# Quadrant layout of B, C and step sizes, one tile for masked scores, and a gate placed behind the second masks

## The chip, the cores and the metric

The kernel runs on one core of one Trainium2 chip. The metric is the device time of one execution in microseconds, less being better. The five engines are TensorE (PE in the rows, its weight loads PEld), VectorE (DVE), ScalarE (ACT), GpSimd (POOL) and SyncE (SP, which here only issues DMAs). They run side by side and are ordered by semaphores alone.

## The reference, cut to what matters

Token ids (64 sequences of 128) pick rows of a quantised embedding table. Then comes one block: a layer norm, an RMS norm, an input projection, a causal convolution of four taps, a scan over time, a gate, an output projection and an MLP. An int8-like linear layer ends it. All data is float32. The change is in the mixer of the block:

```
proj = x @ in_proj_w.T
zgate, u, Bc, Cc, dt = split(proj, [512, 1024, 1040, 1056])     # B, C: 16 wide, dt: 8 heads
u, Bc, Cc = silu(causal_conv4(u, Bc, Cc) + conv_b)
Bc, Cc = l2_normalised(Bc), l2_normalised(Cc)
dt = softplus(dt + dt_bias)
step: z = (z + d*(u B - A y)) / (1 + d*d*A);  y = y + d*z;  out = y . C
yout = (out + D_skip * u) * silu(zgate);  yout @ out_proj_w.T + out_proj_b
```

The scan is computed as a masked matrix product per sequence and head: queries times keys gives scores, the scores are masked to be causal, and their product with u is the output.

## The kernel before, in words

A first part streams the table through on-chip memory to find its quantisation scales (about the first 184 us). The middle part, where the change lies, works on 16 groups of G = 4 sequences (TOK = 512 tokens). A last part multiplies by the int8-like weights.

The middle part is a software pipeline of 18 turns, written out by hand per engine (`pe_turn`, `act_turn`, `dve_turn`, `pool_turn`; turns 2 to 14 are a loop). Turn g works on three groups at once: "first" is group g (normalise, project, recurrence), "second" is p = g-1 (scores, masks, scan output, gate, output projection), "third" is m = g-2 (MLP, residual). Every engine executes its list in order, so an instruction that waits holds up all that stands behind it.

What the change touches, with the lines of the profile:

- `pe_small` (a call of `project`, L600): one product with 40 weight columns (16 B, 16 C, 8 dt) and 512 tokens, for each of two 128-row halves of the contraction. The result is 40 partitions by 512 in `tb[0]`.
- `act_small_in` (L614, L616, L617), `act_small_dt` (L621, L623), `act_small_silu` (L627, L629), `act_small_norm` (L633), `act_small_rsqrt` (L638, L640) on ScalarE, and `dve_conv_small` (L649), `dve_d` (L661), `dve_bc` (L669 to L675) on VectorE: the convolution, softplus and normalisation of these rows, on 32 or 8 partitions by 512.
- `pe_ss` (L654): a product with `norm_sum` that sums squares over the 16 states, 512 columns wide.
- `sp_replicate` (L684 to L703): SyncE writes step sizes to HBM (`scan_rows`), reads them back spread over partitions (`d_rep`, 8 DMAs), then does the same for B and C (8 DMAs each). `act_rep` (L714) turns `d_rep` into X, for which the recurrence on GpSimd waits (`pool_recurrence`, L739 and L741, 64 steps of two instructions, in two halves; between the halves GpSimd computes norm factors from the statistics of L537 and L540).
- After the recurrence ScalarE squares its states (`act_squares`, L748), VectorE makes keys and queries (`dve_keys` from L762, `dve_inverse`, `dve_queries` up to L814), and TensorE makes scores (`pe_scores`, L919) for two half sets of four heads, hg = 0 and hg = 1.
- `dve_mask` (L930) multiplies the scores of one head by the causal mask into the tile `MT`; `pe_scan_out` (L944) multiplies it with u, in pairs of heads. `dve_gate` (L951 and L956) adds the skip and multiplies by the gate, for two 128-channel tiles at a time.
- Behind it on VectorE stand: `dve_row_stats` (L537, L540), `dve_gate` of tiles 2 and 3, `dve_mean3`, `dve_bc`, the convolution of u (`dve_conv_u`, L843), `dve_rms_rows` (L574), the residual `dve_x2` (L973) and `dve_rms` (L989 to L1005). ScalarE scales with that (`act_rms_rows`, L1016), and TensorE transposes the result (`pe_mlp_T`, L1022), goes on to `pe_small`, and then to the MLP (`pe_fc1` L1040 with `act_gelu` L1050, `pe_fc2` L1059).
- GpSimd adds the residual between two recurrences (`pool_residual`, L1069 and L1073).

The order on VectorE around the gate, before:

```
if second:
    dve_gate(dve, p, (0, 1))
    for hh in range(4):
        dve_mask(dve, p, 1, hh)
if nxt:
    dve_row_stats(dve, g + 1)
if second:
    dve_gate(dve, p, (2, 3))
```

Of the kernel before, what the change touches and what calls it, by code (L numbers as in the profile page):

```python
# [28 lines left out]
F32 = mybir.dt.float32  # L29
# [7 lines left out]
G = 4  # L37
# [5 lines left out]
FT = FF // P  # L43
SMALL = 2 * NST + HEADS
TAPS = 4
# [40 lines left out]
def build(nc, a, out):  # L86
    with ExitStack() as ctx:
# [326 lines left out]
        lnst = sb("lnst", [P, 8, G])  # L414
        bc = sb("bc", [SMALL, TOK])
        bsq = sb("bsq", [SMALL, TOK])
        nrm = sb("nrm", [2 * NST, TOK])
        bcd = sb("bcd", [SMALL, TOK])
        X2 = sb("X2", [P, CL, 2, LANES])
# [24 lines left out]

        scan_rows = nc.dram_tensor("scan_rows", (SMALL, TOK), F32, kind="Internal").ap()

# [161 lines left out]
        BC = slice(0, 2 * NST)  # L608
        DT = slice(2 * NST, SMALL)

        def act_small_in(act, g):
            ps = tb[0]
            act.wait_ge(small_mm.sem, small_mm.at(g))
            act.activation(bc[BC, :], ps[BC, :], ACT.Identity, bias=c("bc_bias", 0, BC), scale=c("bc_tap", TAPS - 1, BC)) \  # L614
                .then_inc(tap0.sem, 1)
            act.activation(bc[DT, :], ps[DT, :], ACT.Identity, bias=c("dt_bias", 0, DT)).then_inc(dt_in.sem, 1)  # L616
            act.activation(bsq[DT, :], ps[DT, :], ACT.Abs, bias=c("dt_bias", 0, DT)).then_inc(dt_in.sem, 1)  # L617

        def act_small_dt(act, g):
            act.wait_ge(dt_in.sem, dt_in.at(g))  # L620
            act.activation(bsq[DT, :], bsq[DT, :], ACT.Exp, scale=-1.0).then_inc(dt_act.sem, 1)  # L621
            act.wait_ge(dt_act.sem, dt_act.at(g, 1))
            act.activation(bsq[DT, :], bsq[DT, :], ACT.Ln, bias=1.0).then_inc(dt_act.sem, 1)  # L623

        def act_small_silu(act, g):
            act.wait_ge(cv.sem, cv.at(g))
            act.activation(bc[BC, :], bc[BC, :], ACT.Silu).then_inc(bc_silu.sem, 1)  # L627
            act.wait_ge(bc_silu.sem, bc_silu.at(g))
            act.activation(bsq[BC, :], bc[BC, :], ACT.Square).then_inc(bc_sq.sem, 1)  # L629

        def act_small_norm(act, g):
            act.wait_ge(ss_mm.sem, ss_mm.at(g))
            act.activation(bsq[BC, :], tb[1][BC, :], ACT.Identity, bias=c("eps6", 0, BC)).then_inc(nrm_act.sem, 1)  # L633

        def act_small_rsqrt(act, g):
            act.preload_act_table_set("natural_log_exp_and_others")
            act.wait_ge(nrm_act.sem, nrm_act.at(g, 1))
            act.activation(nrm[:], bsq[BC, :], ACT.Ln).then_inc(nrm_act.sem, 1)  # L638
            act.wait_ge(nrm_act.sem, nrm_act.at(g, 2))
            act.activation(nrm[:], nrm[:], ACT.Exp, scale=-0.5).then_inc(nrm_act.sem, 1)  # L640

        def dve_conv_small(dve, g):
            ps = tb[0][BC, :].rearrange("p (s t) -> p s t", s=G)
            acc = bc[BC, :].rearrange("p (s t) -> p s t", s=G)
            dve.wait_ge(tap0.sem, tap0.at(g))
            for i in range(1, TAPS):
                if i > 1:
                    dve.wait_ge(cv.sem, cv.at(g, i - 1))
                dve.scalar_tensor_tensor(acc[:, :, i:], ps[:, :, 0:LEN - i], c("bc_tap", TAPS - 1 - i, BC),  # L649
                                         acc[:, :, i:], ALU.mult, ALU.add).then_inc(cv.sem, 1)  # L650

        def pe_ss(pe, g):
            pe.wait_ge(bc_sq.sem, bc_sq.at(g))
            pe.matmul(tb[1][:, :], norm_sum[:], bsq[BC, :], start=True, stop=True).then_inc(ss_mm.sem, 1)  # L654

        def dve_d(dve, g):
            if since(g):

                dve.wait_ge(d_stored.sem, d_stored.at(g - 1))
            dve.wait_ge(dt_act.sem, dt_act.at(g))  # L660
            dve.scalar_tensor_tensor(bcd[DT, :], bc[DT, :], 0.0, bsq[DT, :], ALU.max, ALU.add) \  # L661
                .then_inc(d_ready.sem, 1)

        def dve_bc(dve, g):
            if since(g):
                dve.wait_ge(bc_stored.sem, bc_stored.at(g - 1))

            dve.wait_ge(nrm_act.sem, nrm_act.at(g))
            dve.scalar_tensor_tensor(bcd[BC, :], nrm[:], -0.5, nrm[:], ALU.mult, ALU.mult).then_inc(nrm_dve.sem, 1)  # L669
            dve.wait_ge(nrm_dve.sem, nrm_dve.at(g, 1))  # L670
            dve.tensor_tensor(bcd[BC, :], bsq[BC, :], bcd[BC, :], ALU.mult).then_inc(nrm_dve.sem, 1)
            dve.wait_ge(nrm_dve.sem, nrm_dve.at(g, 2))
            dve.scalar_tensor_tensor(nrm[:], bcd[BC, :], 1.5, nrm[:], ALU.add, ALU.mult).then_inc(nrm_dve.sem, 1)
            dve.wait_ge(nrm_dve.sem, nrm_dve.at(g, 3))
            dve.tensor_tensor(bcd[BC, :], bc[BC, :], nrm[:], ALU.mult).then_inc(bc_ready.sem, 1)  # L675

        def sp_replicate(sp, g):

            sp.wait_ge(d_ready.sem, d_ready.at(g))
            if since(g):  # L680

                sp.wait_ge(d_in.sem, d_in.at(g - 1))
                sp.wait_ge(x_ready.sem, x_ready.at(g - 1))
            sp.dma_start(scan_rows[DT, :], bcd[DT, :]).then_inc(d_stored.sem, 16)  # L684
            sp.wait_ge(d_stored.sem, d_stored.at(g))
            for hg in range(HG):
                for head in range(4):
                    row = 2 * NST + 4 * hg + head
# [6 lines left out]
            sp.dma_start(scan_rows[BC, :], bcd[BC, :]).then_inc(bc_stored.sem, 16)  # L695
            sp.wait_ge(bc_stored.sem, bc_stored.at(g))
            if since(g):

                sp.wait_ge(bk_ready.sem, bk_ready.at(g - 1))
                sp.wait_ge(kq.sem, kq.at(g - 1))  # L700
            for rep, row, arrived in ((b_rep, 0, b_in), (c_rep, NST, c_in)):
                for k in range(P // NST):
                    sp.dma_start(rep[k * NST:(k + 1) * NST, :], scan_rows[row:row + NST, :]).then_inc(arrived.sem, 16)  # L703

# [514 lines left out]
        def dve_turn(dve):  # L1219
            def turn(g, first, second, third, nxt):  # L1220
# [418 lines left out]
```

## Time and profile before

| What | Value |
|---|---|
| median of 3 runs | 1486.99 us (1486.4 to 1487.03) |
| the profiled execution, its own time | 1489.13 us |
| its span | 1487.3 us |
| TensorE busy | 1203.7 us (81%) |
| VectorE busy | 1205.1 us (81%) |
| ScalarE busy | 809.2 us (54%) |
| GpSimd busy | 848.8 us (57%) |
| mean granted TensorE clock | 0.932 of full speed |

The profiled execution took 1.8 us more than its span, and 2.1 us more than the median. A row of a timeline has the start in us, the time from there to the end of the last instruction merged into it, the engine, the line, the operation, output and inputs with their shapes, how many instructions, and in brackets the idle time ahead of it with what ended it. TensorE executes each float32 product as two matmul records, so the count in such a row is twice that of the calls.

### The profile page before, as it was taken

What the parts mean: (1) busy time and instruction counts of PE and PEld (TensorE: products, weight loads), DVE (VectorE), ACT (ScalarE), POOL (GpSimd) and SP (SyncE); (2) the same over time, 40 slices, a digit from 0 to 9 for tenths busy, and PEclk for the clock granted to TensorE, in tenths of its full rate; (3) what the DMA queues carried; (4) which work ended last, traced back from release to release, by engine and by line L of the source; (5) the groups of instructions that cost most, each with busy time, mean ns of one, the idle gap of its engine ahead of it and who ended that gap; (6) DMA issues with size and microseconds to landing.
All of it is one profiled execution on the core that took longest, in us unless ns stands there. A gap on an engine that the chain in (4) does not pass through costs nothing. (4 is left out here: it accounts for less than half of the span.)

```text
span 1487.3 us, 24635 instructions
## 1 busy us (share of the span) xinstructions
PE 1203.7 (81%) x6751; PEld 794.8 (53%) x6758; DVE 1205.1 (81%) x2087; ACT 809.2 (54%) x1108; POOL 848.8 (57%) x2326
## 2 busy tenths in 40 slices
PE   0693043498989999989999989999999999998767
PEld 0352011356575656565657565656566665657444
DVE  4899833688888888888888888888898988878268
ACT  4667253355647473838383838374747465641248
POOL 7860027575757576665757575757575757570100
PEclk9999987599999999999999999999999999999889
DMA  9999300000000010101000000000000000000015
GB/s 364 407 408 425 132 18 14 15 17 16 17 14 22 9 30 0 30 2 29 7 23 12 18 16 15 16 15 16 15 16 15 16 15 16 16 17 1 0 37 189
DMA packets 33811, 91.34 MB, mean 61 GB/s; under 512 B 8973, under 2 KB 17922, under 8 KB 29298
## 3 DMA queue, kind: packets, MB, share of 16 engines
q1 hardware_dynamic: 30226, 81.32, 15.4%
q0 software_dynamic: 3072, 8.39, 1.5%
q10 hardware_dynamic: 480, 1.24, 0.2%
q8 instruction: 15, 0.25, 0.1%
q14 instruction: 18, 0.15, 0.0%
HBM read 81.21 MB, written 9.70 MB: 61 GB/s over the span
## 5 line engine op out<-in xcount | busy, mean ns | idle before, releaser
L739 POOL TENSOR_TENSOR stp<-Gs,X 128x32 f32<-128x32 f32 x1024 | 290.3, 284 | 266.4 <-ACT X L714 176.7
L741 POOL TENSOR_TENSOR Gs<-Gs,stp 128x32 f32<-128x32 f32 x1024 | 298.2, 291 | 80.3
L600 PE MATMUL bank<-xT,w_in 128*128 128x512 f32 (+1 forms) x576 | 266.6, 609 | 15.0 <-DVE uT L843 8.2
L1059 PE MATMUL bank<-w_fc,gl 128*128 128x256 f32 x1024 | 238.0, 380 | 13.5 <-ACT gl L1050 13.5
L1040 PE MATMUL bank<-mT,w_fc 128*128 128x512 f32 x512 | 237.9, 603 | 1.5 <-ACT mT L1028 1.5
L1059 PEld LDWEIGHTS bank<-w_fc,gl 128*128 128x128 f32 x1024 | 192.2, 190 | 78.2 <-issue 30.1
L829 ACT ACTIVATE uT<-bank,cols 128x512 f32<-128x512 f32 x64 | 49.4, 776 | 251.6 <-PE bank L600 251.6
L600 PEld LDWEIGHTS bank<-xT,w_in 128*128 128x128 f32 (+1 forms) x576 | 103.0, 186 | 139.5 <-issue 117.4
L1040 PEld LDWEIGHTS bank<-mT,w_fc 128*128 128x128 f32 x512 | 95.6, 191 | 112.4 <-issue 106.9
L944 PE MATMUL bank<-MT,utok 128*64 128x128 f32 x1024 | 111.9, 409 | 45.5 <-DVE MT L930 45.5
L843 DVE SCALAR_TENSOR_TENSOR uT<-bank,cols,uT 128x500 f32<-128x500 f32 (+1 forms) x192 | 134.4, 730 | 2.3
L339 DVE TENSOR_TENSOR peak<-ring,peak 128x1536 f32<-128x1536 f32 (+2 forms) x67 | 115.4, 1722 | 19.9 <-ACT ring L242 18.5
L944 PEld LDWEIGHTS bank<-MT,utok 128*64 128x64 f32 x1024 | 103.5, 224 | 49.9 <-DVE MT L930 44.9
L1050 ACT ACTIVATE gl<-bank,cols 128x512 f32<-128x512 f32 x128 | 84.7, 684 | 76.3 <-PE bank L1059 67.9
L930 DVE TENSOR_TENSOR MT<-bank,causal 128x512 f32<-128x512 f32 x128 | 79.5, 683 | 49.3 <-PE bank L919 49.3
L242 ACT ACTIVATE ring<-ring 128x3072 f32<-128x3072 f32 (+3 forms) x35 | 90.8, 2598 | 51.8 <-DMA ring<-in_table 51.8
L965 PE MATMUL bank<-w_out,sz 128*128 128x256 f32 x512 | 113.8, 380 | 0.2 <-DVE sz L956 0.2
L965 PEld LDWEIGHTS bank<-w_out,sz 128*128 128x128 f32 x512 | 97.2, 190 | 20.7 <-issue 7.5
L807 DVE RECIPROCAL rm<-rm 128x1024 f32<-128x1024 f32 x16 | 104.6, 6540 | 0.0
L280 PE MATMUL bank<-ts,hot 4*128 4x256 f32 x128 | 60.4, 648 | 40.6 <-ACT hot L253 39.2
L226 POOL DMA_INDIRECT h<-in_table,ids x64 | 79.7, 1246 | 19.9 <-issue 19.2
L919 PE MATMUL bank<-Qf,Kf 32*128 32x64 f32 x2048 | 68.0, 283 | 19.7 <-ACT utok L889 13.0
(169 smaller groups left out, 1971.1 us busy)
## 6 DMA issues: line engine op xcount, KB each, us to landing
ring<-in_table SPq DMA_DIRECT2D x32, 1536.0 KB, 21.3
d_rep<-scan_rows SPq DMA_DIRECT2D x128, 64.0 KB, 2.0
out<-res SPq DMA_DIRECT2D x16, 512.0 KB, 2.9
b_rep<-scan_rows SPq DMA_DIRECT2D x128, 32.0 KB, 1.8
c_rep<-scan_rows SPq DMA_DIRECT2D x128, 32.0 KB, 1.8
w_fc<-in_w_fc SPq DMA_DIRECT2D x2, 1024.0 KB, 8.8
w_in<-in_w_in ACTq DMA_DIRECT2D x1, 1064.0 KB
h<-in_table,ids POOLq DMA_INDIRECT x64, 10.1
```

The costliest lines, as they stand in the source:

```text
L242: act.activation(ring[n % RING][0:np_, 0:nr, :], ring[n % RING][0:np_, 0:nr, :], ACT.Abs) \
L339: return dve.tensor_tensor(acc, ring[t][0:np_, r0:r0 + nr, :], acc, ALU.max)
L600: last = pe.matmul(dst, w_in[:, k, c0:c1], xT[:, k, :], start=(k == 0), stop=(k == KD - 1))
L739: pool.tensor_tensor(stp[:], Gs[:, t, ::-1, :], X2[:, t, :, :], ALU.mult).then_inc(rec.sem, 1)
L741: pool.tensor_tensor(Gs[:, t + 1, :, :], Gs[:, t, :, :], stp[:], ALU.add).then_inc(rec.sem, 1)
L807: dve.reciprocal(rm[:], rm[:]).then_inc(inverted.sem, 1)
L843: dve.scalar_tensor_tensor(acc[:, :, i:], ps[:, :, 0:LEN - i], c("u_tap", f * TAPS + TAPS - 1 - i), acc[:, :, i:], ALU.mult, ALU.add).then ...
L944: last = pe.matmul(pj[head // 2][64 * (head % 2):64 * (head % 2) + 64, j * LEN:(j + 1) * LEN], utok[:, j, head * HP:(head + 1) * HP], MT[h ...
L965: last = pe.matmul(sbk[n][:, (j % 2) * D:(j % 2 + 1) * D], sz[:, f, j * LEN:(j + 1) * LEN], w_out[:, f, :], start=(f == 0), stop=(f == UT ...
L1040: last = pe.matmul(pj[n % 4][:, :], w_fc1[:, k, n * P:(n + 1) * P], mT[:, k, :], start=(k == 0), stop=(k == KD - 1))
L1050: act.activation(gl[n % LEAD][:], pj[n % 4][:, :], ACT.Gelu_apprx_tanh, bias=c("fc1_bias", n)) \
L1059: last = pe.matmul(sbk[j // 2][:, (j % 2) * D:(j % 2 + 1) * D], gl[n % LEAD][:, j * LEN:(j + 1) * LEN], w_fc2[:, n, :], start=(n == 0 and ...
```

## The change

B, C and dt of the four sequences are put on four groups of 32 partitions, so that every tile of this chain is 128 partitions by 128 tokens instead of 32 (or 8) by 512. The projection is issued per sequence, once for the 32 columns of B and C and once for 32 columns of which 8 are dt and 24 are zeros: 16 calls of 128 columns instead of 2 of 512. The HBM buffers are laid out by sequence, so that DMAs move runs of 512 bytes instead of 2 KB. The four masked score tiles become one tile with the heads side by side. On VectorE the gate of tiles 0 and 1 moves behind the masks of the second half set.

```
-SMALL = 2 * NST + HEADS
+SMALL = 2 * NST
-        w_in = sb("w_in", [P, KD, 2 * DIN + SMALL])
+        w_in = sb("w_in", [P, KD, 2 * DIN + 2 * SMALL])
-        norm_sum = sb("norm_sum", [2 * NST, P])
+        norm_sum = sb("norm_sum", [P, P])
-        bc = sb("bc", [SMALL, TOK])
...
+        bc = sb("bc", [P, LEN])
...
-        MT = [sb(f"MT{i}", [P, G, LEN]) for i in range(4)]
+        MT = sb("MT", [P, G, 4, LEN])
-        scan_rows = nc.dram_tensor("scan_rows", (SMALL, TOK), F32, kind="Internal").ap()
+        bc_rows = nc.dram_tensor("bc_rows", (G, SMALL, LEN), F32, kind="Internal").ap()
+        d_rows = nc.dram_tensor("d_rows", (G, SMALL, LEN), F32, kind="Internal").ap()
         def pe_small(pe, g):
             pe.wait_ge(xT_ready.sem, xT_ready.at(g))
-            project(pe, tb[0][0:SMALL, :], 2 * DIN, 2 * DIN + SMALL, small_mm.sem)
+            for part in range(2):
+                c0 = 2 * DIN + part * SMALL
+                for k in range(KD):
+                    for j in range(G):
+                        last = pe.matmul(tb[part][SMALL * j:SMALL * (j + 1), 0:LEN],
+                                         w_in[:, k, c0:c0 + SMALL], xT[:, k, j * LEN:(j + 1) * LEN],
+                                         start=(k == 0), stop=(k == KD - 1), skip_group_check=True)
+            last.then_inc(small_mm.sem, 1)
-            act.activation(bsq[BC, :], bc[BC, :], ACT.Square).then_inc(bc_sq.sem, 1)
+            act.activation(bsq[:], bc[:], ACT.Square).then_inc(bc_sq.sem, 1)
...
-            pe.matmul(tb[1][:, :], norm_sum[:], bsq[BC, :], start=True, stop=True).then_inc(ss_mm.sem, 1)
+            pe.matmul(tb[1][:, LEN:2 * LEN], norm_sum[:], bsq[:], start=True, stop=True).then_inc(ss_mm.sem, 1)
-            sp.dma_start(scan_rows[DT, :], bcd[DT, :]).then_inc(d_stored.sem, 16)
+            sp.dma_start(d_rows.rearrange("j r t -> (j r) t"), dd[:]).then_inc(d_stored.sem, 16)
-                    sp.dma_start(d_rep[32 * head:32 * head + 32, hg, :],
-                                 scan_rows[row:row + 1, :].to_broadcast([32, TOK])).then_inc(d_in.sem, 16)
+                    sp.dma_start(d_rep[32 * head:32 * head + 32, hg, :].rearrange("p (j t) -> p j t", j=G),
+                                 d_rows[:, row:row + 1, :].rearrange("j r t -> r j t").to_broadcast([32, G, LEN])) \
+                        .then_inc(d_in.sem, 16)
...
-            dve.tensor_tensor(MT[hh][:], score_bank[hh][:, :].rearrange("p (j t) -> p j t", j=G),
+            dve.tensor_tensor(MT[:, :, hh, :], score_bank[hh][:, :].rearrange("p (j t) -> p j t", j=G),
...
                 if second:
-                    dve_gate(dve, p, (0, 1))
                     for hh in range(4):
                         dve_mask(dve, p, 1, hh)
+                    dve_gate(dve, p, (0, 1))
                 if nxt:
                     dve_row_stats(dve, g + 1)
```

## Rows read from the trace of the kernel before

**Rows 1.** Page, part 1: busy time, share of the span and instructions.

```profile
PE 1203.7 (81%) x6751; PEld 794.8 (53%) x6758; DVE 1205.1 (81%) x2087; ACT 809.2 (54%) x1108; POOL 848.8 (57%) x2326
```

**Rows 2.** The loop's instruction (L1128) on TensorE: count, duration, first and last start.

```profile
L1128 PEldq ALU_OP  x13: 32/32/32, 384.0 to 1244.2; - x13
```

**Rows 3.** Timeline of TensorE, 865 to 935 us, a turn of the loop.

```profile
868.99 2.01 PE L919 MATMUL bank<-Qf,Kf 32*128 32x64 f32 x64
872.41 3.48 PE L944 MATMUL bank<-MT,utok 128*64 128x128 f32 x32 [1.41 <-DVE MT L930]
...
897.61 1.09 PE L1022 MATMUL bank<-ident,xr 128*128 128x128 f32 x8
899.05 1.91 PE L600 MATMUL bank<-xT,w_in 128*40 128x512 f32 x4 [0.35 <-ACT xT L596]
900.89 7.13 PE L1040 MATMUL bank<-mT,w_fc 128*128 128x512 f32 x16
908.99 1.99 PE L1059 MATMUL bank<-w_fc,gl 128*128 128x256 f32 x8 [0.96 <-ACT gl L1050]
...
921.24 1.12 PE L654 MATMUL bank<-bsq,norm_sum 32*128 32x512 f32 x2
922.29 1.98 PE L1040 MATMUL bank<-mT,w_fc 128*128 128x512 f32 x4
...
933.81 1.46 PE L919 MATMUL bank<-Qf,Kf 32*128 32x64 f32 x44 [0.88 <-ACT utok L889]
```

**Rows 4.** Timeline of VectorE, the same turn.

```profile
871.07 2.48 DVE L930 TENSOR_TENSOR MT<-bank,causal 128x512 f32<-128x512 f32 x4
...
875.42 1.37 DVE L951 SCALAR_TENSOR_TENSOR uT<-uT,cols,bank 128x512 f32<-128x512 f32 x2
876.71 1.29 DVE L956 TENSOR_TENSOR sz<-sz,uT 128x512 f32<-128x512 f32 x2
...
878.74 0.70 DVE L669 SCALAR_TENSOR_TENSOR bcd<-nrm 32x512 f32<-32x512 f32 x1
...
890.08 0.88 DVE L973 SCALAR_TENSOR_TENSOR xl<-bank,off,xl 128x256 f32<-128x256 f32 x2 [0.26 <-PE bank L965]
...
906.97 2.24 DVE L661 SCALAR_TENSOR_TENSOR bcd<-bc,bsq 8x512 f32<-8x512 f32 x1 [0.92 <-ACT bsq L623]
911.35 1.22 DVE L762 TENSOR_TENSOR rm<-utok 128x1024 f32<-128x1024 f32 x1 [2.14 <-ACT utok L748]
...
931.46 1.46 DVE L1081 TENSOR_TENSOR h<-bank,h 128x512 f32 x2
```

**Rows 5.** Timeline of ScalarE, the same turn.

```profile
895.85 1.71 ACT L1016 ACTIVATE xr<-xl,ssq 128x256 f32<-128x256 f32 x4 [1.05 <-DVE ssq L1005]
...
901.00 0.77 ACT L614 ACTIVATE bc<-bank,cols 32x512 f32<-32x512 f32 x1 [0.54 <-PE bank L600]
...
904.37 0.63 ACT L621 ACTIVATE bsq<-bsq 8x512 f32<-8x512 f32 x1
...
908.25 1.27 ACT L1050 ACTIVATE gl<-bank,cols 128x512 f32<-128x512 f32 x2
909.40 1.91 ACT L748 ACTIVATE utok<-Gs 128x2048 f32<-128x2048 f32 x1
```

**Rows 6.** Timeline of GpSimd, the same turn.

```profile
875.59 0.20 POOL L549 TENSOR_TENSOR lnst<-mv,eps 128x4 f32<-128x4 f32 x1 [2.04 <-DVE mv L540]
...
906.32 2.34 POOL L1069 TENSOR_TENSOR h<-h,xl 128x1024 f32 x1 [0.29 <-issue]
908.84 2.61 POOL L1073 TENSOR_TENSOR h<-h,fc_b 128x1024 f32 x1 [0.17 <-issue]
```

**Rows 7.** Timeline of TensorE, 868.3 to 869 us: the last scan-output records.

```profile
867.97 1.10 PE L944 MATMUL bank<-MT,utok 128*64 128x128 f32 x10
```

**Rows 8.** Page, part 6: DMA issues, count, KB each, us to landing.

```profile
d_rep<-scan_rows SPq DMA_DIRECT2D x128, 64.0 KB, 2.0
...
out<-res SPq DMA_DIRECT2D x16, 512.0 KB, 2.9
```

More of the change, by code:

```diff
@@ L414, in build @@
         lnst = sb("lnst", [P, 8, G])
-        bc = sb("bc", [SMALL, TOK])
-        bsq = sb("bsq", [SMALL, TOK])
-        nrm = sb("nrm", [2 * NST, TOK])
-        bcd = sb("bcd", [SMALL, TOK])
+        bc = sb("bc", [P, LEN])
+        bsq = sb("bsq", [P, LEN])
+        nrm = sb("nrm", [P, LEN])
+        bcd = sb("bcd", [P, LEN])
+        dt = sb("dt", [P, LEN])
+        soft = sb("soft", [P, LEN])
+        dd = sb("dd", [P, LEN])
         X2 = sb("X2", [P, CL, 2, LANES])
@@ L611, in act_small_in @@
+            last.then_inc(small_mm.sem, 1)
         def act_small_in(act, g):
[L612 removed]
+            bc_in, dt_raw = tb[0][:, 0:LEN], tb[1][:, 0:LEN]
             act.wait_ge(small_mm.sem, small_mm.at(g))
[L614 removed]
+            act.activation(bc[:], bc_in, ACT.Identity, bias=c("bc_bias"), scale=c("bc_tap", TAPS - 1)) \
                 .then_inc(tap0.sem, 1)
[L616 removed]
@@ L617, in act_small_in @@
-            act.activation(bsq[DT, :], ps[DT, :], ACT.Abs, bias=c("dt_bias", 0, DT)).then_inc(dt_in.sem, 1)
+            act.activation(dt[:], dt_raw, ACT.Identity, bias=c("dt_bias")).then_inc(dt_in.sem, 1)
+            act.activation(soft[:], dt_raw, ACT.Abs, bias=c("dt_bias")).then_inc(dt_in.sem, 1)
         def act_small_dt(act, g):
             act.wait_ge(dt_in.sem, dt_in.at(g))
-            act.activation(bsq[DT, :], bsq[DT, :], ACT.Exp, scale=-1.0).then_inc(dt_act.sem, 1)
+            act.activation(soft[:], soft[:], ACT.Exp, scale=-1.0).then_inc(dt_act.sem, 1)
@@ L622, in act_small_dt @@
             act.wait_ge(dt_act.sem, dt_act.at(g, 1))
-            act.activation(bsq[DT, :], bsq[DT, :], ACT.Ln, bias=1.0).then_inc(dt_act.sem, 1)
+            act.activation(soft[:], soft[:], ACT.Ln, bias=1.0).then_inc(dt_act.sem, 1)
         def act_small_silu(act, g):
             act.wait_ge(cv.sem, cv.at(g))
-            act.activation(bc[BC, :], bc[BC, :], ACT.Silu).then_inc(bc_silu.sem, 1)
+            act.activation(bc[:], bc[:], ACT.Silu).then_inc(bc_silu.sem, 1)
             act.wait_ge(bc_silu.sem, bc_silu.at(g))
-            act.activation(bsq[BC, :], bc[BC, :], ACT.Square).then_inc(bc_sq.sem, 1)
+            act.activation(bsq[:], bc[:], ACT.Square).then_inc(bc_sq.sem, 1)
@@ L637, in act_small_rsqrt @@
             act.wait_ge(nrm_act.sem, nrm_act.at(g, 1))
-            act.activation(nrm[:], bsq[BC, :], ACT.Ln).then_inc(nrm_act.sem, 1)
+            act.activation(nrm[:], bsq[:], ACT.Ln).then_inc(nrm_act.sem, 1)
             act.wait_ge(nrm_act.sem, nrm_act.at(g, 2))
@@ L660, in dve_d @@
             dve.wait_ge(dt_act.sem, dt_act.at(g))
-            dve.scalar_tensor_tensor(bcd[DT, :], bc[DT, :], 0.0, bsq[DT, :], ALU.max, ALU.add) \
+            dve.scalar_tensor_tensor(dd[:], dt[:], 0.0, soft[:], ALU.max, ALU.add) \
                 .then_inc(d_ready.sem, 1)
@@ L668, in dve_bc @@
             dve.wait_ge(nrm_act.sem, nrm_act.at(g))
-            dve.scalar_tensor_tensor(bcd[BC, :], nrm[:], -0.5, nrm[:], ALU.mult, ALU.mult).then_inc(nrm_dve.sem, 1)
+            dve.scalar_tensor_tensor(bcd[:], nrm[:], -0.5, nrm[:], ALU.mult, ALU.mult).then_inc(nrm_dve.sem, 1)
             dve.wait_ge(nrm_dve.sem, nrm_dve.at(g, 1))
-            dve.tensor_tensor(bcd[BC, :], bsq[BC, :], bcd[BC, :], ALU.mult).then_inc(nrm_dve.sem, 1)
+            dve.tensor_tensor(bcd[:], bsq[:], bcd[:], ALU.mult).then_inc(nrm_dve.sem, 1)
             dve.wait_ge(nrm_dve.sem, nrm_dve.at(g, 2))
-            dve.scalar_tensor_tensor(nrm[:], bcd[BC, :], 1.5, nrm[:], ALU.add, ALU.mult).then_inc(nrm_dve.sem, 1)
+            dve.scalar_tensor_tensor(nrm[:], bcd[:], 1.5, nrm[:], ALU.add, ALU.mult).then_inc(nrm_dve.sem, 1)
             dve.wait_ge(nrm_dve.sem, nrm_dve.at(g, 3))
-            dve.tensor_tensor(bcd[BC, :], bc[BC, :], nrm[:], ALU.mult).then_inc(bc_ready.sem, 1)
+            dve.tensor_tensor(bcd[:], bc[:], nrm[:], ALU.mult).then_inc(bc_ready.sem, 1)
         def sp_replicate(sp, g):
@@ L687, in sp_replicate @@
                 for head in range(4):
-                    row = 2 * NST + 4 * hg + head
-                    sp.dma_start(d_rep[32 * head:32 * head + 32, hg, :],
-                                 scan_rows[row:row + 1, :].to_broadcast([32, TOK])).then_inc(d_in.sem, 16)
+                    row = 4 * hg + head
+                    sp.dma_start(d_rep[32 * head:32 * head + 32, hg, :].rearrange("p (j t) -> p j t", j=G),
+                                 d_rows[:, row:row + 1, :].rearrange("j r t -> r j t").to_broadcast([32, G, LEN])) \
+                        .then_inc(d_in.sem, 16)
             sp.wait_ge(bc_ready.sem, bc_ready.at(g))
@@ L694, in sp_replicate @@
                 sp.wait_ge(c_in.sem, c_in.at(g - 1))
-            sp.dma_start(scan_rows[BC, :], bcd[BC, :]).then_inc(bc_stored.sem, 16)
+            sp.dma_start(bc_rows.rearrange("j r t -> (j r) t"), bcd[:]).then_inc(bc_stored.sem, 16)
             sp.wait_ge(bc_stored.sem, bc_stored.at(g))
@@ L702, in sp_replicate @@
                 for k in range(P // NST):
-                    sp.dma_start(rep[k * NST:(k + 1) * NST, :], scan_rows[row:row + NST, :]).then_inc(arrived.sem, 16)
+                    sp.dma_start(rep[k * NST:(k + 1) * NST, :].rearrange("p (j t) -> p j t", j=G),
+                                 bc_rows[:, row:row + NST, :].rearrange("j r t -> r j t")).then_inc(arrived.sem, 16)
         def act_rep(act, g, hgs):
@@ L944, in pe_scan_out @@
                     last = pe.matmul(pj[head // 2][64 * (head % 2):64 * (head % 2) + 64, j * LEN:(j + 1) * LEN],
-                                     utok[:, j, head * HP:(head + 1) * HP], MT[hh][:, j, :], start=True, stop=True)
+                                     utok[:, j, head * HP:(head + 1) * HP], MT[:, j, hh, :], start=True, stop=True)
             last.then_inc(y_mm.sem, 1)
@@ L1598 @@
     cols["norm2"][:] = tall(f["L0_attn_norm2_w"])
-    cols["bc_tap"][0:2 * NST] = taps[DIN:]
-    cols["bc_bias"][0:2 * NST, 0] = f["L0_attn_conv_b"][DIN:]
-    cols["dt_bias"][2 * NST:SMALL, 0] = f["L0_attn_dt_bias"]
+    cols["bc_tap"][:] = np.tile(taps[DIN:], (G, 1))
+    cols["bc_bias"][:, 0] = np.tile(f["L0_attn_conv_b"][DIN:], G)
+    for j in range(G):
+        cols["dt_bias"][SMALL * j:SMALL * j + HEADS, 0] = f["L0_attn_dt_bias"]
     cols["u_tap"][:] = taps[:DIN].reshape(UT, P, TAPS).transpose(1, 0, 2).reshape(P, UT * TAPS)
@@ L1620 @@
         "ident": np.eye(P, dtype=np.float32),
-        "norm_sum": np.kron(np.eye(2, P // NST, dtype=np.float32), np.ones((NST, NST), np.float32)),
+        "norm_sum": np.kron(np.eye(P // NST, dtype=np.float32), np.ones((NST, NST), np.float32)),
         "causal": (s <= t).astype(np.float32),
-        "w_in": wide(f["L0_attn_in_proj_w"].T),
+        "w_in": wide(np.pad(f["L0_attn_in_proj_w"].T, ((0, 0), (0, SMALL - HEADS)))),
         "w_out": wide(f["L0_attn_out_proj_w"].T),
```

10 lines of the change are left out of this document (3 added, 7 removed).

## The prediction

> **What bounds the kernel now.** The page's totals name two candidates, TensorE and VectorE at 81% each [rows 1]. The loop over turns repeats every (1244.2 - 384.0) / 12 = 71.7 us [rows 2], so the 14 turns from 2 to 15 are two thirds of the span, and what one turn gains counts about 14 times. I then read one turn as four timelines side by side. TensorE is almost without gaps: it idles 1.41 us twice (masks, once per half set), 0.35, 0.96 and 0.88 us [rows 3]. So a turn shortens by work taken from TensorE, or by one of these gaps, and lengthens by whatever makes a new one.
>
> Three chains run beside TensorE. (a) From the end of the second scores (868.99 + 2.01 = 871.00) VectorE is dense to the row normalisation; it idles only 0.26 us there, before L973 [rows 4]. ScalarE then scales rows from 895.85 to 897.56 [rows 5], and TensorE transposes them at 897.61 [rows 3]. TensorE shows no gap there, but only 0.05 us separate the two: this chain has no slack. (b) From the small projection ScalarE goes through five small operations to the first gelu at 908.25 [rows 5], and its end at about 908.9 releases L1059 after the 0.96 us gap. (c) The recurrence on GpSimd leads to the squares at 909.40, the keys at 911.35 and h2 at 931.46 [rows 4, 5]. VectorE is done there at 932.9, while the first scores end near 933.81 + 2.01 = 935.8: slack 2.9 us.
>
> **The change, part by part, for one turn.**
>
> *Small projection.* Before: 4 records of 512 columns, 1.84 us from 899.05 to 900.89 [rows 3]. After: 32 records of 128 columns, in four column strips of the array. The nearest row is L944, also 128 columns wide and alternating between two strips: 32 records take 3.48 us, 109 ns each [rows 3]. That is the upper bound, +1.65 us. The lower bound is the rate of L919, where four row strips share the array: 2.01 / 64 = 31 ns a record [rows 3], 1.0 us in all, -0.85 us. I take the middle, 1.9 us, for this reason: ten records of L944 begin at 867.97 and the next line begins at 868.99 [rows 7, 3], 1.02 us, where ten times 109 ns is 1.09 us even without a change of shape between them. So the two strips do overlap at the end of the run, where no weights are left to load; in the stream, loading and multiplying seem to take turns. With four strips that would be four records per 213 ns, or 8 x 0.213 = 1.7 us. I take +0.1.
>
> The Trainium skill (TensorEngine Tiling (Array Packing), Overview) gives up to 4x for stationary operands of at most 32 columns; by that the projection would cost 3.41 / 4 = 0.9 us. Its page TensorE: Matmul & The Clock Gate, Part 3, speaks against the change: weight loads overlap running matmuls only in another row group, and here all rows are used. L944's 109 ns a record agrees with the second, not with the first.
>
> *Sum of squares.* Before 922.29 - 921.24 = 1.05 us [rows 3]. After: two records of 128 columns at 109 ns: 0.22. **-0.83**.
>
> *ScalarE.* An operation of 512 columns takes 0.63 us, one of 256 takes 1.71 / 4 = 0.43 [rows 5], so 384 columns fewer save 0.30 us. Five such operations stand between the small projection and the first gelu: it ends 1.5 us earlier, and the 0.96 us gap goes. **-0.96**. What is late next there is the end of fc1 itself, 0.5 us later than gelu would be. Silu, square, norm and rsqrt lie beside TensorE work; they cost nothing now and give nothing.
>
> *VectorE.* 512 columns take 0.70, 256 take 0.44 [rows 4]: 0.39 saved per operation. The four of `dve_bc` lie in chain (a): -1.56. The three of the small convolution and `dve_d` lie ahead of a wait of 2.14 us for the squares [rows 4] and give nothing.
>
> *The gate.* Masks of the second set start at 871.07, 0.07 us after the scores end: the gate ahead of them was all but hidden in the time TensorE needed for scan output and scores. Moved behind the masks, it leaves VectorE idle there and puts 1.37 + 1.29 = 2.66 us [rows 4] into chain (a). Behind it wait: the row statistics, and through them GpSimd's norm factors, which already idled 2.04 us for them [rows 6]; the second gate, `dve_bc`, the u convolution, L973, the row normalisation. Sum for chain (a): 2.66 - 1.56 - 0.26 (the wait before L973) = **+0.8** as a new gap before L1022. The u projection needs the first gate at 875.9; it would be done at 874.3.
>
> *GpSimd.* Its second half starts 2.6 us later, so the recurrence ends near 908.7, just before ScalarE is free for the squares. But the residual operations of 2.34 and 2.61 us [rows 6] then run from 909.0 to 914.1, over the first keys. That this costs is seen now: `dve_d` takes 2.24 us for 8 x 512 [rows 4] and ends 0.5 us after L1069 does; its size would give 0.70. Two such hits are up to 3.1 us on chain (c), whose slack of 2.9 us is down to 2.8. Bounds 0 and 3.1; I take **+0.3**. The Trainium skill (GPSIMD Engine Reference, Specifications) says that GpSimd and VectorE share their SBUF interface when a VectorE instruction has two SBUF inputs; the 2.24 us agrees.
>
> *DMAs.* On SyncE's queue the counts stay (1 + 8 + 1 + 16). Runs shrink from 2 KB to 512 B, and the step-size store grows from 16 to 64 KB. A replication lands in 2.0 us, a 512 KB store in pieces of 1 KB in 2.9 us [rows 8]; so 0 to 0.9 us more, on a chain that gets over 2 us earlier. Cover: ScalarE's gelus; gone, it would delay X and GpSimd, which has 2.04 us to spare. Nothing. *The MT tile:* same shapes read and written, nothing. *Zero columns and larger norm_sum:* 72 KB more at the start, 0.2 us.
>
> Sum per turn: 0.1 - 0.83 - 0.96 + 0.8 + 0.3 = -0.6; 14 turns: -8.3. Ahead of the first recurrence the small operations lie bare: about -2; the last turns, where the gate delays GpSimd's last recurrence, +1. Total -9: the profiled 1489.1 becomes 1480, the median, 2.1 lower, **1478 us**.
>
> **The rivals.**
>
> 1. *The strips don't overlap.* The projection costs the full 3.5 us: +1.55 on each turn, 14 x 1.55 = 22, so about 1500 us: slower. For it: the 109 ns of L944. Against: rows 7. It decides from 2.5 us for the projection on.
> 2. *Chain (a) does not bind.* If the masks' wait or shorter operations hide the gate, +0.8 and +0.3 vanish: -1.7 per turn, -24, so 1462 us. For it: VectorE's total falls. Against: the 0.05 us of slack.
> 3. *The gate's move eats everything.* VectorE saves less than reckoned and the collision costs 1.0 beyond its slack: 0.1 - 1.79 + 1.2 + 1.0 = +0.5, so 1493 us: slower.
> 4. *Strips in full parallel:* 0.9 us less per turn, 1465 us.
>
> A change of 0.2% (3 us) is what a measurement of this kernel can tell from none.
>
> **How the numbers follow.** Forecast 0.45, its own range 1471 to 1484; rival 1 0.22, rival 2 0.12, rival 3 0.13, rival 4 0.08. Faster by over 0.2%: the forecast's most (0.42), rivals 2 and 4: 0.62. Same: 0.08 (edges of the forecast and of rival 3). Slower: 0.30. The range takes in most of rivals 2 and 4 and half of rival 1: 1463 to 1500.
>
> **What the profile after would show.** The projection in 1.9 us or less (3.5 by rival 1); the sum of squares in 0.3; no gap before the first L1059; a new gap of 0.8 us before L1022, with VectorE idle near 3 us before the second masks; GpSimd waiting over 4 us for the statistics; its residual beside L762. I am wrong if the period is not near 71.1 us: above 71.7 by rivals 1 or 3, near 70 by rival 2.

## The result and the profile after

The changed kernel takes 1504.75 us in the median of four runs (1504.15 to 1508.39), the kernel before 1486.7 us. The ratio is 1.0128 (95% interval 1.0113 to 1.0143): slower by 18 us, where 9 us less were forecast, and outside the range by 5 us.

The page, parts 1 and 6, and one group of part 5 of the changed kernel (its profiled execution took 1508.39 us, span 1506.5 us):

```profile
PE 1200.8 (80%) x7199; PEld 828.4 (55%) x7206; DVE 1161.0 (77%) x2087; ACT 759.5 (50%) x1108; POOL 822.8 (55%) x2326
...
L927 PE MATMUL bank<-Qf,Kf 32*128 32x64 f32 x2048 | 95.3, 357 | 41.4 <-DVE h L1089 34.0
...
d_rep<-d_rows SPq DMA_DIRECT2D x128, 64.0 KB, 2.7
```

Every engine works less than in [rows 1], VectorE by 44 us (only TensorE's weight loads, PEld, grew, by 34 us), and yet the time grew. The loop's own instruction repeats (after the count the shortest, the median and the longest duration in ns, then the first and the last start in us):

```profile
L1136 PEldq ALU_OP  x13: 32/32/32, 376.9 to 1257.8; - x13
```

(1257.8 - 376.9) / 12 = 73.4 us against 71.7 [rows 2]. These twelve periods hold 20.7 us of the loss. The stretch ahead of them got 7.1 us shorter (2 were forecast), the one behind them 5.6 us longer (1 was forecast), and together that is the 19.2 us between the spans. The length of the first scores of a turn (L919 before, L927 now) was not in the forecast: they now wait for "DVE h L1089", the result of the MLP added to h (h2 in the prediction), and the mean record of all scores grew from 283 to 357 ns. The timeline of TensorE over one turn answers to [rows 3]:

```profile
642.75 3.19 PE L927 MATMUL bank<-Qf,Kf 32*128 32x64 f32 x64 [2.45 <-DVE h L1089]
647.33 3.35 PE L952 MATMUL bank<-MT,utok 128*64 128x128 f32 x32 [1.39 <-DVE MT L938]
...
679.82 1.09 PE L1030 MATMUL bank<-ident,xr 128*128 128x128 f32 x8 [0.67 <-ACT xr L1024]
681.27 1.08 PE L614 MATMUL bank<-xT,w_in 128*32 128x128 f32 x32 [0.36 <-ACT xT L600]
682.81 7.13 PE L1048 MATMUL bank<-mT,w_fc 128*128 128x512 f32 x16 [0.46 <-ACT mT L1036]
689.77 1.89 PE L1067 MATMUL bank<-w_fc,gl 128*128 128x256 f32 x8
...
701.83 0.39 PE L660 MATMUL bank<-bsq,norm_sum 128*128 128x128 f32 x2
702.05 1.88 PE L1048 MATMUL bank<-mT,w_fc 128*128 128x512 f32 x4
...
715.06 3.69 PE L927 MATMUL bank<-Qf,Kf 32*128 32x64 f32 x64 [2.47 <-DVE h L1089]
```

The turn of before that it is read against begins with two lines ahead of [rows 3]:

```profile
862.14 2.01 PE L919 MATMUL bank<-Qf,Kf 32*128 32x64 f32 x64 [0.91 <-ACT utok L889]
865.56 3.50 PE L944 MATMUL bank<-MT,utok 128*64 128x128 f32 x32 [1.41 <-DVE MT L930]
```

Read from start to start, the stretches differ so: first scores to first scan output +1.2 us, on to the transposes of L1030 +0.4 (in it the 0.67 us gap), projection -0.3 net of a new gap of 0.46, fc1 up to the first fc2 -1.1, sum of squares -0.8, the rest up to the next scores +1.3. Sum +0.6: this turn takes 72.3 us, where those of before take 71.7. Five turns of the loop take 74.4 to 74.8 us and one 73.8; in the five, the second scores take 3.69 us as well.

One more comparison shows where TensorE's saving went. From the end of the second scores to the end of h2's addition (L1081 before, L1089 now) it is 932.92 - 871.00 = 61.9 us before and 714.82 - 652.61 = 62.2 now. The side that TensorE waits for has not become shorter, so what TensorE saves on the way stands as a wait before the scores.

What VectorE and GpSimd do in the same turn, answering to [rows 4] and [rows 6]:

```profile
652.68 2.48 DVE L938 TENSOR_TENSOR MT<-bank,causal 128x512 f32<-128x512 f32 x4 [2.72 <-PE bank L927]
...
691.21 1.23 DVE L770 TENSOR_TENSOR rm<-utok 128x1024 f32<-128x1024 f32 x1 [3.83 <-ACT utok L756]
692.35 3.25 DVE L775 TENSOR_TENSOR Kf<-bk,Gs 128x512 f32<-128x512 f32 x1
...
713.54 1.28 DVE L1089 TENSOR_TENSOR h<-bank,h 128x512 f32 x2
```

```profile
659.71 0.20 POOL L553 TENSOR_TENSOR lnst<-mv,eps 128x4 f32<-128x4 f32 x1 [5.75 <-DVE mv L544]
...
688.85 2.36 POOL L1077 TENSOR_TENSOR h<-h,xl 128x1024 f32 x1 [0.29 <-issue]
691.39 3.25 POOL L1081 TENSOR_TENSOR h<-h,fc_b 128x1024 f32 x1 [0.17 <-issue]
```

VectorE stands idle 2.72 us ahead of the second masks, where the gate was. GpSimd waits 5.75 us for the statistics behind the gate. Its second residual addition runs from 691.39 to 694.64, and the key operation L775 from 692.35 to 695.60: both take 3.25 us. Alone they take 2.36 (the median in the run with the gate put back, below) and 1.1. The key operation ends 0.96 us after the addition does. L1089 ends at 714.8, and the scores start at once.

The last view is the granted clock in chosen stretches, first of the kernel before, then of the changed one (after the stretch and its length: busy time of PE, PEld, DVE, ACT and POOL, the granted clock, DMA share and GB/s):

```profile
865.60:868.90 3.30, 3.30 (x32) 3.22 (x32) 3.16 (x7) 0.00 (x0) 2.53 (x10) 0.52 0.00 0
869.00:871.00 2.00, 2.00 (x66) 1.87 (x64) 1.89 (x3) 0.00 (x0) 1.69 (x5) 1.00 0.00 0
```

```profile
642.75:645.90 3.15, 3.15 (x64) 3.00 (x64) 0.00 (x0) 0.20 (x1) 2.40 (x10) 0.60 0.00 0
```

In the kernel before, the scores (from 869.0) ran at the full 2.4 GHz, but the scan output in front of them, which follows a wait of 1.41 us, at 1.2 GHz. I had priced the new projection by just such a row, and had not asked for its clock. In the changed kernel, behind the wait of 2.45 us, the scores run at the low level for most of their time too: 3.19 us where 2.01 [rows 3] do at full clock.

Over twelve turns of the loop (first scores at 432.2 to first scores at 1292.0 us before, 424.4 to 1305.2 now) this gives, per turn, from the timelines and the clock record:

| Per turn | before | changed |
|---|---|---|
| period | 71.65 us | 73.39 us |
| TensorE's waits over 0.1 us | 5.0 us | 6.7 us |
| of these, before the first scores | 0.88 us | 2.47 us |
| of these, before L1022 / L1030 | 0 | 0.53 us (0.16 to 1.14) |
| first scores | 2.01 us | 3.31 us (2.67 to 3.69) |
| second scores | 2.01 us | 2.79 us (3.69 in five of twelve) |
| time at the low clock | 6.8 us | 13.1 us |

So the clock costs the two sets of scores 2.1 us a turn, which is more than the 1.6 us that the waits add.

### The profile page after: what moved, and what is told of

The parts are those of the page before. It is cut to its first block and busy times, and to the rows that moved or that the text cites. A ratio compares the mean times of both kernels' runs of the same rounds, so it can differ in the third digit from the quotient of the medians.

```text
span 1506.5 us, 25531 instructions
## 1 busy us (share of the span) xinstructions
PE 1200.8 (80%) x7199; PEld 828.4 (55%) x7206; DVE 1161.0 (77%) x2087; ACT 759.5 (50%) x1108; POOL 822.8 (55%) x2326
## 5 line engine op out<-in xcount | busy, mean ns | idle before, releaser
L747 POOL TENSOR_TENSOR stp<-Gs,X 128x32 f32<-128x32 f32 x1024 | 281.5, 275 | 240.7 <-DVE Kf L812 140.3
L749 POOL TENSOR_TENSOR Gs<-Gs,stp 128x32 f32<-128x32 f32 x1024 | 284.2, 278 | 80.3
L604 PE MATMUL bank<-xT,w_in 128*128 128x512 f32 x512 | 237.3, 612 | 7.8 <-DVE uT L851 7.4
L604 PEld LDWEIGHTS bank<-xT,w_in 128*128 128x128 f32 x512 | 98.0, 197 | 118.5 <-issue 105.0
L927 PE MATMUL bank<-Qf,Kf 32*128 32x64 f32 x2048 | 95.3, 357 | 41.4 <-DVE h L1089 34.0
L952 PEld LDWEIGHTS bank<-MT,utok 128*64 128x64 f32 x1024 | 99.4, 216 | 51.7 <-DVE MT L938 46.8
L927 PEld LDWEIGHTS bank<-Qf,Kf 32*128 32x128 f32 x2048 | 90.0, 266 | 49.7 <-issue 49.7
L553 POOL TENSOR_TENSOR lnst<-mv,eps 128x4 f32<-128x4 f32 x16 | 3.3, 203 | 172.5 <-DVE mv L544 172.5
```

What stands on the lines that cost most here:

```text
L604: last = pe.matmul(dst, w_in[:, k, c0:c1], xT[:, k, :], start=(k == 0), stop=(k == KD - 1))
L747: pool.tensor_tensor(stp[:], Gs[:, t, ::-1, :], X2[:, t, :, :], ALU.mult).then_inc(rec.sem, 1)
L749: pool.tensor_tensor(Gs[:, t + 1, :, :], Gs[:, t, :, :], stp[:], ALU.add).then_inc(rec.sem, 1)
L927: last = pe.matmul(score_bank[hh][:, t:t + CL], Kf[own, hg * G + j, ch * CL:ch * CL + P], Qf[own, hg, t:t + CL], start=True, stop=True)
```

## The experiments

Three questions: which part of the change costs, through which chain, and what share the clock has. Ratios are to the kernel before, with their 95% intervals.

### The parts, one at a time

The changed kernel with the gate put back:

```
-                    for hh in range(4):
-                        dve_mask(dve, p, 1, hh)
                     dve_gate(dve, p, (0, 1))
+                    for hh in range(4):
+                        dve_mask(dve, p, 1, hh)
```

> The changed kernel with the gate of tiles 0 and 1 put back ahead of the second masks; quadrant layout and single mask tile stay. Theory A (the moved gate is what costs: it delays the statistics, GpSimd's recurrence and its residual, which then runs over the keys, so that the scores wait 2.5 us for h2): faster than before, 1465 to 1480 us, the gap before the first scores under 1.5 us, L1030 without a gap. Rival B (the layout alone does it: TensorE gets through its part 2.5 us sooner and merely waits for a VectorE chain that was nearly as long, at half clock afterwards): 1487 to 1505 us, the gap before the scores still 2 us or more.

1465.85 us, ratio 0.9862 (0.9838 to 0.9887), as by theory A: in its timeline the first scores wait 0.88 us (2.1 in one turn), and L1030 has no gap. The kernel before with this one move made, in the other direction:

> The kernel before with only the gate moved behind the second masks. Theory A: the shortening of the normalisation is missing, so about 2.3 us before the transposes of L1022, and about 1.3 us more before the scores from the collision: 1487 + 14 x 3.6 = about 1535 us (1520 to 1545). Rival B: the gate costs little by itself, under 1 us per turn, 1487 to 1500 us.

1533.02 us, ratio 1.032 (1.0295 to 1.0345). In its timeline the transposes of L1022 wait, and run slowly behind the wait:

```profile
769.85 1.60 PE L1022 MATMUL bank<-ident,xr 128*128 128x128 f32 x8 [2.02 <-ACT xr L1016]
771.38 3.05 PE L600 MATMUL bank<-xT,w_in 128*40 128x512 f32 x4
```

That is 2.0 us of wait and 0.5 + 1.1 us of low clock (granted 0.64 and 0.62 in the two stretches) against [rows 3], together 3.6 per turn, as expected in sum; the period grows by 3.3, from 71.65 to 74.99 us. But the collision I expected is not there (its scores wait 0.88 us as before). Without the shorter ScalarE operations the keys start at 784.80 and GpSimd's residual has ended at 783.96. The sum was right and one of its two terms was not.

The kernel before with the single mask tile only (`MT = sb("MT", [P, G, 4, LEN])`, and the two lines that use it):

> The kernel before with only the single mask tile. Both theories: no effect, 1487 us within 0.2%, masks of 683 ns each as before. If the strided writes cost anything, the masks are longer and so are the gaps of 1.41 us before the scan output.

1486.56 us, ratio 0.9999 (0.9989 to 1.0008), masks of 684 ns on the mean: nothing, as forecast. The kernel before with the quadrant layout only (the diff of the change without `MT` and without the move):

> The kernel before with only the quadrant layout of B, C and step sizes. As the run with the gate put back, within 0.2% of it, if the mask tile does nothing: 1465 to 1480 us by theory A, 1487 to 1505 by rival B.

1462.27 us, ratio 0.9842 (0.9826 to 0.9859). So the layout gives 24 us and the mask tile nothing. The moved gate takes 39 us on top of the layout (1504.75 - 1465.85) and 46 in the kernel before. The run with the gate put back and this one should be the same kernel but for the mask tile; they lie 3.6 us apart, 0.24% where 0.2% was expected, with intervals that meet.

The layout could give more. In 8 of its twelve turns the second scores take 3.69 us, and such turns last 71.2 to 71.5 us; the others, where they take 2.01, last 68.9.

### Through which chain the gate costs

In the changed kernel, statistics taken ahead of the moved gate:

```
                     for hh in range(4):
                         dve_mask(dve, p, 1, hh)
-                    dve_gate(dve, p, (0, 1))
                 if nxt:
                     dve_row_stats(dve, g + 1)
+                if second:
+                    dve_gate(dve, p, (0, 1))
```

> The changed kernel with the row statistics taken ahead of the moved gate (still behind the second masks). This parts the two prices of the move. Theory A1 (late statistics are the price: GpSimd's residual falls on the keys, and the scores wait for h2): the statistics come 2.7 us sooner, L1077 starts near where L1069 did against its turn, no key operation of 3.25 us, the wait for h2 before the first scores falls from 2.47 us to under 1.2, the time comes to within 10 us of 1466. Rival A2 (the longer VectorE chain up to L1030 is the price): this chain is as long as in the changed kernel, so the time stays above 1490 us.

1481.25 us, ratio 0.9963 (0.9946 to 0.9979), between the two expectations. Its executions differ more than those of any other kernel here (1466.88 to 1485.49), and the profiled one is the fastest, so its rows flatter it:

```profile
647.80 7.13 PE L604 MATMUL bank<-xT,w_in 128*128 128x512 f32 x16 [0.20 <-DVE uT L959]
...
669.81 1.09 PE L1030 MATMUL bank<-ident,xr 128*128 128x128 f32 x8 [0.22 <-ACT xr L1024]
...
703.65 2.16 PE L927 MATMUL bank<-Qf,Kf 32*128 32x64 f32 x64 [1.08 <-DVE h L1089]
```

The wait for h2 is down from 2.47 to 1.08 us. The gate, now later still, holds up the u projection by 0.2 to 0.6 us. The order alone returned 23 us of the 39. No key operation takes 3.25 us here, as expected (L775 takes 1.10 in the median), but the operation ahead of it, L770, takes 1.98 us in most turns of the loop instead of 1.22: the collision is smaller and has not gone.

The same statistics in VectorE's idle time ahead of the second masks (`dve_row_stats(dve, g + 1)` above the loop of masks), the gate where the change puts it:

> The changed kernel with the row statistics in the idle time of VectorE ahead of the second masks; the gate stays behind them. By either theory both prices of the moved gate go: no gap before L1030, no collision, 1462 to 1470 us as with the gate put back. If a late gate costs by itself (through the u projection, which waits for it), the time stays above 1475 us.

1466.6 us, ratio 0.986 (0.9843 to 0.9876), as expected. The whole loss is gone with the gate still behind the masks. A late gate is not dear; what it keeps waiting is.

Then the collision itself. The changed kernel with the two residual additions of GpSimd cut to 4 columns. It leaves out the rest of the residual and of the second MLP bias:

> The changed kernel with GpSimd's two residual additions cut from 1024 to 4 columns; the rest of the residual and of the second MLP bias is left out. Theory A1 (the collision of these additions with the first keys is what makes the scores late): the key operation of 3.25 us takes 1.1 us, the wait before the first scores falls from 2.47 to about 0.9 us, 1462 to 1480 us. Rival A2 (the longer chain up to L1030 is the price): over 1490 us.

1458.85 us, ratio 0.9806 (0.9785 to 0.9827), 3 us below the range of theory A1 and far from A2. TensorE in one turn of it:

```profile
703.12 2.01 PE L927 MATMUL bank<-Qf,Kf 32*128 32x64 f32 x64 [0.88 <-ACT utok L897]
...
738.87 1.09 PE L1030 MATMUL bank<-ident,xr 128*128 128x128 f32 x8 [1.10 <-ACT xr L1024]
```

and the same line in the turn before:

```profile
669.47 1.09 PE L1030 MATMUL bank<-ident,xr 128*128 128x128 f32 x8 [0.17 <-ACT xr L1024]
```

VectorE:

```profile
681.98 1.08 DVE L775 TENSOR_TENSOR Kf<-bk,Gs 128x512 f32<-128x512 f32 x1
```

L775 takes 1.08 us instead of 3.25, the first scores no longer wait for h2 and run at full clock, and 46 us go. The gap before L1030 stays: it is 0.15 to 1.10 us from turn to turn, and sums to 6.4 us over the twelve turns, just as in the changed kernel. The period is 70.5 us, that of the run with the gate put back. So in the kernels without fillers the collision, with the low clock behind its wait, is the larger price of the move, and the long VectorE chain the smaller. One control is missing: the same cut with the gate in its old place. The layout alone has a small hit too (L770 takes 1.3 to 1.6 us in most turns and 2.5 to 2.9 in two), so a part of the 46 us may come without the move.

### The clock

The quadrant layout alone, with products of no use in TensorE's waits:

```
+        def pe_filler(pe, p, m, n):
+            pe.wait_ge(z_ready.sem, z_ready.at(p))
+            if since(p):
+                pe.wait_ge(gelu.sem, gelu.at(p - 1))
+            pe.matmul(pj[3][:, 0:n], ident[:], w_fc1[:, 0, 0:n], start=True, stop=True)
...
+                    pe_filler(pe, p, m, 384)
                     for hg in range(HG):
                         pe_scores(pe, p, hg)
+                        pe_filler(pe, p, m, 512)
+                        pe_filler(pe, p, m, 256)
                         pe_scan_out(pe, p, hg, 0)
```

> The kernel with only the quadrant layout, with products of no use (128 rows, 384, 512 and 256 columns, their results overwritten by the scan output) in TensorE's waits before the first scores and before each scan output. Theory C (the turns of 71.2 us differ from those of 68.9 us only by stretches at half clock behind these waits): full clock through the turn, all turns near 68.9 us or less, 1435 to 1448 us. Rival: the fillers only take the place of waits and push the real work, 1462 us or more.

1437.77 us, ratio 0.9686 (0.9665 to 0.9708). More work, 24.5 us less time, as by theory C. Without the products (the run above):

```profile
706.56 3.68 PE L952 MATMUL bank<-MT,utok 128*64 128x128 f32 x32 [1.41 <-DVE MT L938]
710.17 3.69 PE L927 MATMUL bank<-Qf,Kf 32*128 32x64 f32 x64
715.27 3.68 PE L952 MATMUL bank<-MT,utok 128*64 128x128 f32 x32 [1.41 <-DVE MT L938]
```

With them:

```profile
691.76 2.01 PE L927 MATMUL bank<-Qf,Kf 32*128 32x64 f32 x64 [1.47 <-DVE h L1095]
693.70 1.56 PE L946 MATMUL bank<-w_fc,ident 128*128 128x512 f32 x4
695.19 2.28 PE L958 MATMUL bank<-MT,utok 128*64 128x128 f32 x32
697.39 2.01 PE L927 MATMUL bank<-Qf,Kf 32*128 32x64 f32 x64
699.34 1.56 PE L946 MATMUL bank<-w_fc,ident 128*128 128x512 f32 x4
701.57 2.29 PE L958 MATMUL bank<-MT,utok 128*64 128x128 f32 x32 [0.68 <-DVE MT L938]
```

The granted clock from 695.3 to 697.4 is 1.00 here:

```profile
695.30:697.40 2.10, 2.01 (x33) 1.60 (x34) 2.01 (x5) 0.00 (x0) 1.55 (x8) 1.00 0.00 0
```

The same 32 records of the scan output take 2.28 us at 2.4 GHz and 3.68 at 1.2 (granted 0.50 from 706.6 to 710.2): 71 and 115 ns a record. The fillers cost the waits they stand in, and the clock pays them back. The collision with GpSimd's residual is in this kernel as well, with the gate in its old place:

```profile
736.95 2.97 DVE L770 TENSOR_TENSOR rm<-utok 128x1024 f32<-128x1024 f32 x1 [3.81 <-ACT utok L756]
```

L770 takes 1.22 us alone, and 2.95 us in the median of this run.

The kernel before with the same products:

> The kernel before with products of no use in TensorE's waits before the first scores and before each scan output. Theory C (L944 takes 3.5 us for 32 records only because these stretches run at 1.2 GHz): 32 records take about 2.3 us at the full clock, VectorE's masks and gate then bind between the scores, some 1.5 us less per turn, 1455 to 1472 us. Rival: L944 takes 3.5 us at full clock as well, 1487 us or more.

1472.3 us, ratio 0.9905 (0.9889 to 0.9922), 0.3 us above the range; the period falls by 0.8 us, from 71.65 to 70.83, and not by 1.5. L950, its scan output, takes 2.28 us too, and what it gains shows partly as new waits (0.68 us for masks, 0.82 for the row normalisation). The changed kernel with them:

> The changed kernel with the same products in the same waits. Theory C: the clock only makes the waits dearer; without its part the moved gate costs what the waits cost by themselves, about 1.3 us per turn against 1437.8 us: 1450 to 1462 us. Rival: the waits before L1030 and for h2, which no product fills, bring the half clock back all the same, 1475 us or more.

1472.89 us, ratio 0.9911 (0.9895 to 0.9928), above what I expected and below the rival. Two waits that no filler covers stay:

```profile
706.94 2.01 PE L927 MATMUL bank<-Qf,Kf 32*128 32x64 f32 x64 [1.79 <-DVE h L1095]
...
741.74 1.09 PE L1036 MATMUL bank<-ident,xr 128*128 128x128 f32 x8 [1.09 <-ACT xr L1030]
```

With the scans at full clock in both kernels, the moved gate still costs 1472.9 - 1437.8 = 35 us. Here the collision does not explain it, since both kernels have one (2.97 us for L770 there, 3.25 for L775 here). Over the twelve turns, where the two differ by 26.3 us, the waits before L1036 add 13.0 us (1.09 us in nearly every turn, none in the other kernel), those of the u projection for the late gate 4.5, those for h2 4.2, and 6.7 us of waits for masks fall away. That is 15 us. The low clock holds 34 us of these turns against 14, but how the remaining 11 us divide was not measured. So with the clock filled up, the longer VectorE chain is the larger price and the collision the smaller.

### Two smaller ones

The order of the small projection, strip by strip instead of round the strips (loop over j outside the loop over k):

> The kernel with only the quadrant layout, the 16 products of the small projection issued strip by strip (both halves of the contraction of one strip behind each other). If the 1.08 us for 32 records comes from neighbours in different strips running side by side, this order takes 1.7 us or more; if it comes from the narrow weights alone, 1.08 us again.

1467.06 us in one run, and its records are the same (count, shortest, median and longest duration in ns, first and last start in us of each kernel's L614; the first fence is the layout alone, the second the strip-by-strip order):

```profile
L614 PE MATMUL bank<-xT,w_in x512: 272/273/421, 191.9 to 1234.8; 128*32 128x128 f32 x171
```

```profile
L614 PE MATMUL bank<-xT,w_in x512: 272/273/422, 191.5 to 1233.6; 128*32 128x128 f32 x171
```

The 32 records take 1.12 us in the timeline, against 1.08, so a row of the code need not alternate strips. By the expectation this speaks for the narrow weights alone, but the starts of the single records speak against it. The windows view counts the records that lie in a stretch, those still running included. In the changed kernel (after the stretch and its length: busy time of PE and of PEld with their records, clock, DMA):

```profile
681.30:681.40 0.10, 0.10 (x4) 0.10 (x8) 1.00 0.00 0
681.40:681.43 0.03, 0.03 (x8) 0.03 (x8) 1.00 0.00 0
681.43:681.50 0.07, 0.07 (x8) 0.07 (x4) 1.00 0.00 0
681.50:681.54 0.04, 0.04 (x12) 0.04 (x8) 1.00 0.00 0
```

and in the strip-by-strip order:

```profile
669.91:669.96 0.05, 0.05 (x8) 0.05 (x4) 1.00 0.00 0
669.97:670.02 0.05, 0.05 (x12) 0.05 (x8) 1.00 0.00 0
670.02:670.07 0.05, 0.05 (x12) 0.05 (x4) 1.00 0.00 0
```

In both orders four records start close together, and the next four 0.11 us later. 0.11 us is also what one record of 128 columns takes on the undivided array: eight in 675.55 - 674.67 = 0.88 us (L591 in the changed kernel, and the start of the line behind it). So four run at the same time. Which strip each record belongs to, the trace does not say.

The filled version with the layer norm moved into VectorE's idle time ahead of the keys:

> The quadrant layout with filled waits (1437.8 us), and VectorE's layer norm (1.65 us, L907) moved into its idle time ahead of the keys. Theory: the chain from the squares to h2 binds there (wait of 1.47 us before the first scores), so it gets up to 1 us shorter: 1423 to 1432 us. Rival: the layer norm meets GpSimd's residual in that place and pushes the keys, 1437 us or more.

1435.21 us, ratio 0.9654 (0.9638 to 0.967), between the two expectations. The rival's mechanism took nearly all of the gain:

```profile
737.34 3.69 DVE L907 SCALAR_TENSOR_TENSOR xl<-h,rs,out_b 128x256 f32<-128x256 f32 x4 [3.48 <-POOL h L1083]
```

Waiting for GpSimd's first residual addition, the four operations run into the second and take 3.69 us instead of 1.65. It is the fastest kernel of this study, 51 us under the one before, though its interval meets that of the version without the move.

## Why the prediction was wrong, point by point

- **Small projection, +0.1 forecast, -0.8 measured** (1.84 to 1.08 us). The step that failed is the reading of L944's 109 ns a record as a price at full clock; rows 7, from which the four records per 213 ns come, lie where that stretch of low clock ends (granted 0.62 from 867.97 to 868.99). It was a price at 1.2 GHz, as the stretch at 0.52 above shows; at 2.4 GHz it is 71 ns. The rival "strips in full parallel" was right: 34 ns a record. The 4x of the Trainium skill (TensorEngine Tiling (Array Packing), Overview), 0.9 us by estimate, was nearer than my sum. The rule of the Trainium skill that I set against it (TensorE: Matmul & The Clock Gate, Part 3), that weight loads overlap only in other row groups, did not hold the four strips back here: 32 loads and 32 products passed in 1.08 us.
- **Sum of squares, -0.83 forecast and measured** (0.22 us from start to start).
- **First gelu, -0.96 forecast.** The gap is gone, but fc1 now waits 0.46 us for mT, because the projection ahead of it no longer covers ScalarE's copies: -0.5 net. I named the end of fc1 as what is late next, and it was its start.
- **Chain (a), +0.8 forecast, 0.5 measured** as the gap before L1030 (the mean of twelve turns; 0.67 in the turn shown). Right in its mechanism, with VectorE idle 2.72 us ahead of the second masks as described.
- **GpSimd and chain (c), +0.3 forecast, +1.6 measured** as wait before the first scores (2.47 us for 0.88): this step failed, and its low clock below belongs to it. The collision came where it was expected, with 2.15 us on the first keys. But its slack was read off the end of the first scores (2.9 us), and the scores themselves wait for h2 before they start: L1081 ended at 932.9, the scores began at 933.8 [rows 3, 4], slack 0.9 us. And I did not take from that slack what TensorE saves between the transposes and the scores, by measurement 2.3 us (0.29 + 1.14 + 0.83). Savings on the one side of a meeting point are waits there as long as the other side does not move.
- **The clock, put at nothing.** Behind the longer wait the first scores run at the low clock for most of their time: +0.7 to +1.7 us in every turn of the loop, +1.3 on the mean. In five of the twelve turns the second scores follow at 3.69 us, +0.8 on the mean. Together +2.1, the largest term of all, and the forecast had none for it. This is behind the third rival's shortfall too: the collision did eat everything (1493 us forecast), but its size was wrong, and VectorE did save what was reckoned (0.40 us per operation of `dve_bc`, for 0.39).
- **DMAs and mask tile, nothing forecast.** The mask tile is shown by its own run. A replication lands in 2.7 us instead of 2.0, inside the bound of 0.9, and no wait on it is among the causes found.

In sum per turn: -0.6 was forecast, +1.7 came.

What stays open: how the 39 us of the gate divide between collision and chain (a). The order of the statistics returns 23 us, removing the residual 46, and both change the clock as well; the effects do not add, and with fillers the order of the two prices is turned round.

## What to carry to other kernels

Before a row prices a new operation, ask for the granted clock of that row's stretch: behind a wait of 1.4 us it may be half. For each chain find the first instruction that waits for its end, not a later one, and charge the slack with what the other side saves. An engine's work moved out of an idle stretch into a dense one costs its full length, and everything queued behind it, on other engines too, arrives later at places where it may meet something.

## What the runs showed of the hardware that was not expected

- TensorE's waits of 1.4 us are mostly, though not always, followed by stretches at 1.2 GHz (the scan output behind such a wait takes 3.68 us both times in the turn shown of the quadrant layout, 3.23 and 2.29 us in that of the run without the residual), and useless products in them make the whole kernel 1.7% faster (1462.27 to 1437.77 us; the kernel before 1.0%, to 1472.3).
- Four products in column strips run side by side in float32: 32 records of 128 columns in 1.08 us at full clock, and in 1.12 us when the calls to one strip follow each other, where the undivided array takes 0.11 us for each.
- A VectorE operation with two inputs in on-chip memory and a GpSimd addition of 1024 columns hold each other up (3.25 us for 1.1, and 3.25 for 2.36). The VectorE operation ends about its own length after the addition ends: 0.96 us for L775 (1.1 alone), 1.47 for the four of L907 (1.65 alone). The Trainium skill (GPSIMD Engine Reference, Specifications) has the shared interface; the trace agrees, and without the addition the operation takes 1.08 us.
